# One pool of seven PSUM banks, handed out by the plan, in place of a ring of four and a ring of three

## The reference

```
h = layernorm(x) * (1 + ca) + sa
x = x + ga * attention(h)       # 16 heads of 16, causal, softmax
h = layernorm(x) * (1 + cb) + sb
x = x + gb * ffn(h)
```

## Time and profile before

| what | value |
|---|---|
| runs | 2794.85, 2794.88, 2792.37 us; median 2794.85 |
| the profiled execution: its own time | 2790.14 us |
| its span, first to last instruction | 2788.4 us |
| mean granted TensorE clock | 0.961 |
| instructions | 55137 |
| PE / DVE / ACT / POOL busy | 2464.7 / 2156.4 / 1711.5 / 1025.8 us |

### The profile page before, as it was taken

One profiled execution on the slowest core, in us unless ns is written; L12 is line 12 of the kernel. 1 busy time (PEld: TensorE's weight loads), 2 busy tenths in 40 slices (PEclk: granted clock), 3 DMA queues, 4 the chain that ended last, 5 costly groups with the idle time before them and its releaser, 6 DMA issues.

```text
span 2788.4 us, 55137 instructions
## 1 busy us (share of the span) xinstructions
PE 2464.7 (88%) x18968; PEld 1027.6 (37%) x18968; DVE 2156.4 (77%) x6588; ACT 1711.5 (61%) x3458; POOL 1025.8 (37%) x1558
## 2 busy tenths in 40 slices
PE   6898888988999999988999989999999989897686
PEld 4323333423334343343434333443433434333223
DVE  3897758788887988878887988878888788872961
ACT  3475575555765667756675666656677566664264
POOL 4222542244242443335243442434433352335222
PEclk9999999999999999999999999999999999998788
DMA  6510143121413222311423214131223114004000
GB/s 213 171 58 20 37 130 99 34 80 48 139 48 101 62 89 83 111 49 50 122 67 93 77 53 139 54 104 51 88 83 111 49 50 136 21 29 136 30 2 16
DMA packets 142394, 218.29 MB, mean 78 GB/s; under 512 B 21190, under 2 KB 62556, under 8 KB 142052
## 3 DMA queue, kind: packets, MB, share of 16 engines
q1 hardware_dynamic: 142120, 214.77, 25.5%
HBM read 137.87 MB, written 77.89 MB: 77 GB/s over the span
## 4 chain that ended last, share of the span: by engine, by line
PE 54%; DVE 24%; ACT 10%; issue 5%; POOL 5%; DMA 1%; SPq 0%; DVEq 0%; POOLq 0%; ACTq 0%
PE ctx_ps L1649 11%; PE big L1630 11%; PE big L1567 10%; DVE small L1398 8%; PE big L1556 8%; PE small L1608 7%; ACT probs L1184 6%; DVE mx L1396 4%; PE big L1681 4%; ACT xn L1233 4%; DVE stats L1352 3%; PE big L1664 2%; DVE region L1461 2%; DVE mx L1398 1%; DVE region L1499 1%
## 5 line engine op out<-in xcount | busy, mean ns | idle before, releaser
L1184 ACT ACTIVATE probs<-big 128x512 f32<-128x512 f32 (+2 forms) x2560 | 1221.4, 563 | 429.9 <-PE big L1630 421.4
L1398 DVE CUSTOM_DVE_ANT_0 small<-small,mask 128x128 f32<-128x128 f32 (+3 forms) x2048 | 942.9, 520 | 141.6 <-PE small L1608 130.7
L1630 PE MATMUL big<-stack_q,stack_k 64*128 64x512 f16 (+3 forms) x6144 | 711.8, 330 | 81.1 <-ACT probs L1184 52.8
L1396 DVE TENSOR_REDUCE mx<-small 128x1 f32<-128x512 f32 x1024 | 652.1, 682 | 102.8 <-PE small L1608 96.5
L1649 PE MATMUL ctx_ps<-probs,v_ones 128*17 128x512 f32 (+3 forms) x6144 | 646.6, 498 | 28.8 <-POOL probs L1063 19.3
L1063 POOL TENSOR_SCALAR_AFFINE_SELECT probs<-probs 128x512 f32<-128x512 f32 x512 | 329.0, 653 | 674.4 <-ACT probs L1184 674.1
L1608 PE MATMUL small<-stack_k,stack_q 64*128 64x512 f16 (+3 forms) x3072 | 458.0, 335 | 130.9 <-DVE mx L1398 76.0
L1630 PEld LDWEIGHTS big<-stack_q,stack_k 64*128 64x128 f16 x6144 | 232.0, 95 | 610.5 <-issue 356.5
L1608 PEld LDWEIGHTS small<-stack_k,stack_q 64*128 64x128 f16 x3072 | 128.9, 94 | 549.6 <-DVE mx L1398 248.7
L1398 DVE DVE_READ_ACCUMULATOR2_ANT mx<- 128x1 f32 x2048 | 286.2, 140 | 0.0
L1556 PE MATMUL big<-hT,w_qkv 128*128 128x512 f32 x512 | 274.3, 640 | 1.5 <-ACT probs L1184 1.4
(11 more groups left out here) (94 smaller groups left out, 1938.6 us busy)
## 6 DMA issues: line engine op xcount, KB each, us to landing
image<-region SPq DMA_DIRECT2D x192, 256.0 KB
stack_q<-image SPq DMA_DIRECT2D x64, 512.0 KB, 3.8
stack_k<-image SPq DMA_DIRECT2D x64, 512.0 KB, 4.7
lo_dram<-region SPq DMA_DIRECT2D x64, 256.0 KB
w_qkv<-wqkv SPq DMA_DIRECT2D x16, 768.0 KB, 6.4
x_res<-x SPq DMA_DIRECT2D x32, 256.0 KB, 3.5
stack_q<-lo_dram SPq DMA_DIRECT2D x128, 64.0 KB, 4.2
stack_k<-lo_dram SPq DMA_DIRECT2D x128, 64.0 KB, 5.2
```

Source lines behind the costliest of these rows:

```text
L1184: s.activation(probs[:, n % HELD, heads, q0:], big[:, at.slot(turn), 0:len(pairs) * width] .rearrange("p (h q) -> p h q", h=len(pairs)), A ...
L1396: last = v.reduce_max(to, held, AX)
L1398: last = v.tensor_tensor_reduce(out=held, in0=held, in1=mask[:, BANK - width:], scale=1.0, scalar=3.0 * NEG, op0=ALU.add, op1=ALU.max, acc ...
L1630: last = te.matmul(big[:, at.slot(at.turn() + parity), j * width:(j + 1) * width], stack_k[rows, c, g * PAIR_N + pair, kt * P:(kt + 1) * P ...
```

## The change

`big` becomes one PSUM tensor of seven banks, and `small` is a view of its last three, used by the start-up items alone. The plan chooses the bank of every turn and every `max` bank use: of those open, the one whose last reader ends first in the model. Turns may use all seven once the first `max` step has been placed. In the model a turn still waits until no more than three turns are unread before it, and a `max` use until no more than two (`MOST`); the kernel itself waits for the chosen bank alone. All banks have a `freed` semaphore, so a `max` step on PE waits for two semaphores where it waited for one, and the `join` on DVE waits for each bank that the group's last uses had. The constant `DMA_NS` is changed, and the pulls of `max`, `pre` and `post` get an addend by phase (`PHASES`: four groups in each of two layers; five values are not zero), so the order of the items changes as well.

```diff
-RING = 4
-SMALL = 3
+BANKS = 7
+ONCE_BANKS = 3
+MOST = {"turn": 4, "max": 3}
...
-SEEN, DMA_NS = 232.7037, 466.9094
+SEEN, DMA_NS = 232.7037, 407.8548
...
+PHASES = {"max": (0.0000, 0.0000, 0.0000, 0.0000, 0.0000, 0.0000, 0.0000, 0.0000), "pre": (-0.0748, 0.0000, 0.1675, 0.0000, 0.0000, 0.0000, 0.0000, 0.0000), "post": (0.0397, 0.0000, 0.0000, -0.2876, 0.0000, 0.0000, 0.0000, -0.0889)}
...
+    def open_to(self, use):
+        return range(BANKS if self.taken["max"] else BANKS - ONCE_BANKS) if use == "turn" else range(BANKS)
+
+    def bank_free(self, use, n=1):
+        own, first = self.ends[use], MOST[use] - n + 1
+        return max(sorted(self.banks[b] for b in self.open_to(use))[n - 1], own[-first] if len(own) >= first else 0.0)
+
+    def take_bank(self, use):
+        b = min(self.open_to(use), key=lambda b: self.banks[b])
+        self.taken[use].append((b, self.used[b]))
+        self.used[b] += 1
+        self.banks[b] = 1e18
+        return b
...
-            return max(own, self.ring[self.turn % RING], self.ring[(self.turn + 1) % RING])
+            return max(own, self.bank_free("turn", 2))
...
-            return max(self.at(("stack", unit, item[2])), self.small[self.step % SMALL], self.small[(self.step + 1) % SMALL])
+            return max(self.at(("stack", unit, item[2])), self.bank_free("max", 2))
...
+        phase = 4 * UNITS[scores[0][1]][1] + scores[0][2] if scores else 7
...
-            return cost - PULL[name] * (done * all_[name] - taken[name] + AHEAD[name] * all_[name] / N_UNITS)
+            ahead = AHEAD[name] + (PHASES[name][phase] if name in PHASES else 0.0)
+            return cost - PULL[name] * (done * all_[name] - taken[name] + ahead * all_[name] / N_UNITS)
...
-        return (self.turn() if turn is None else turn) % RING
+        return MODEL.taken["turn"][self.turn() if turn is None else turn][0]
...
-        return turn // RING
+        return MODEL.taken["turn"][turn][1]
...
-        return (self.own("max") + parity) % SMALL
+        return MODEL.taken["max"][self.own("max") + parity]
...
-        big = ctx.enter_context(nc.psum_tensor("big", [P, RING, BANK], f32))
+        big = ctx.enter_context(nc.psum_tensor("big", [P, BANKS, BANK], f32))
+        small = big[:, BANKS - ONCE_BANKS:]
...
-                    dve.wait_ge(s_freed, at.now("max", SMALL))
+                    for bank, use in dict(MODEL.taken["max"][:at.own("max")][-GROUP_STEPS:]).items():
+                        dve.wait_ge(freed[bank], use + 2)
...
-                    pe.wait_ge(s_freed, at.now("max", 2))
+                    for parity in range(2):
+                        bank, use = at.max_bank(parity)
+                        pe.wait_ge(freed[bank], use + 1)
```

More of the change, by code:

```diff
@@ L84, in piece_width @@
     return BANK if qt // 4 > blk else (qt % 4 + 1) * P
+GROUP_STEPS = 2 * PAIR_N * len(MAX_BANKS)
 LN_CHAIN, LN_GUESS = 18, 4
@@ L228, in __init__ @@
         self.free = {"PE": 0.0, "ACT": 0.0, "DVE": 0.0, "POOL": 0.0, "SP": 0.0}
-        self.ring, self.small, self.shape = [0.0] * RING, [0.0] * SMALL, None
-        self.turn = self.step = 0
+        self.banks, self.used, self.shape = [0.0] * BANKS, [0] * BANKS, None
+        self.taken, self.ends, self.opened = {"turn": [], "max": []}, {"turn": [], "max": []}, None
         self.ready, self.pipe = {}, 0.0
@@ L252, in needs @@
         if kind == "half":
-            return max(self.needs(item[2]), self.ring[self.turn % RING])
+            return max(self.needs(item[2]), self.bank_free("turn"))
         if kind == "score":
@@ L260, in needs @@
         if kind == "max":
-            return max(self.at(("stack", unit, item[2])), self.small[self.step % SMALL], self.small[(self.step + 1) % SMALL])
+            return max(self.at(("stack", unit, item[2])), self.bank_free("max", 2))
         if kind == "rows":
-            return max(self.at(("join", unit, item[2])), self.ring[self.turn % RING])
+            return max(self.at(("join", unit, item[2])), self.bank_free("turn"))
         own = {"proj": [("ctx", unit), ("scale", unit)], "turned": [("xn", unit)], "qk": [("h", unit), ("pre_loads", unit)], "value": [("h", unit)],
                "gate": [("mix", unit)], "key": [("mix", unit)], "y": [("h", unit), ("square", unit), ("scale", unit), ("bias", unit, 3)]}[kind]
-        bank = 0.0 if item in self.ready else self.ring[self.turn % RING]
+        bank = 0.0 if item in self.ready else self.bank_free("turn")
         return max(self.at(*own), bank)
@@ L334, in bank @@
     def bank(self, end):
-        self.ring[self.turn % RING] = end
-        self.turn += 1
+        b = self.take_bank("turn") if self.opened is None else self.opened
+        self.opened, self.banks[b] = None, end
+        self.ends["turn"].append(end)
     def play(self, item):
@@ L346, in play @@
             self.ready[item[2]] = 0.0
+            self.opened = self.take_bank("turn")
             self.free["PE"] = begin + pe_cost(item[2]) / 2
@@ L364, in play @@
                 cost = sum(piece_width(qt, blk) * 1.04 + 75 for qt, blk, _ in item[4])
-                self.small[self.step % SMALL] = self.run("DVE", end + SEEN, cost)
-                self.step += 1
+                b = self.take_bank("max")
+                self.banks[b] = self.run("DVE", end + SEEN, cost)
+                self.ends["max"].append(self.banks[b])
         elif kind == "rows":
@@ L685, in slot, with max_bank @@
     def slot(self, turn=None):
-        return (self.turn() if turn is None else turn) % RING
+        return MODEL.taken["turn"][self.turn() if turn is None else turn][0]
     def uses(self, turn):
-        return turn // RING
-    def small(self, parity):
-        return (self.own("max") + parity) % SMALL
+        return MODEL.taken["turn"][turn][1]
+    def max_bank(self, parity):
+        return MODEL.taken["max"][self.own("max") + parity]
     def done(self, item):
@@ L800, in adaln_program @@
         w_lin = w_ffn[:, 2]
-        big = ctx.enter_context(nc.psum_tensor("big", [P, RING, BANK], f32))
+        big = ctx.enter_context(nc.psum_tensor("big", [P, BANKS, BANK], f32))
+        small = big[:, BANKS - ONCE_BANKS:]
         ctx_ps = ctx.enter_context(nc.psum_tensor("ctx_ps", [P, BANK], f32))
-        small = ctx.enter_context(nc.psum_tensor("small", [P, SMALL, BANK], f32))
         c_in = sem("c_in")
@@ L824, in adaln_program @@
         filled = sem("filled")
-        freed = [sem(f"freed_{i}") for i in range(RING)]
+        freed = [sem(f"freed_{i}") for i in range(BANKS)]
         s_filled = sem("s_filled")
-        s_freed = sem("s_freed")
         xn_ready = sem("xn_ready")
@@ L1263, in _ @@
                 dve.sem_inc(bank, 1)
-            dve.sem_inc(s_freed, SMALL)
             dve.sem_inc(pv_done, HELD)
@@ L1392, in step @@
                             width = piece_width(qt, blk)
-                            held = small[:, at.small(parity), col:col + width]
+                            held = big[:, at.max_bank(parity)[0], col:col + width]
                             to = mx[:, g % 2, (parity * PAIR_N + pair) * NT + qt, blk:blk + 1]
@@ L1400, in step @@
                                     scale=1.0, scalar=3.0 * NEG, op0=ALU.add, op1=ALU.max, accum_out=to)
-                        last.then_inc(s_freed, 1)
+                        last.then_inc(freed[at.max_bank(parity)[0]], 1)
                 elif kind == "join":
                     g = item[2]
-                    dve.wait_ge(s_freed, at.now("max", SMALL))
+                    for bank, use in dict(MODEL.taken["max"][:at.own("max")][-GROUP_STEPS:]).items():
+                        dve.wait_ge(freed[bank], use + 2)
                     v.tensor_tensor(mxc[:, g % 2, :], mx[:, g % 2, :, 0], mx[:, g % 2, :, 1], ALU.max)\
@@ L1607, in step @@
                             rows = rows_of(parity)
-                            last = te.matmul(small[:, at.small(parity), col:col + width],
+                            last = te.matmul(big[:, at.max_bank(parity)[0], col:col + width],
                                              stack_q[rows, 0, g * PAIR_N + pair, qt * P:(qt + 1) * P],
```

## The result

| kernel | median us | runs | ratio to before, 95% interval |
|---|---|---|---|
| before | 2793.61 | 4 | |
| changed | 2745.93 (2741.7 to 2751.26) | 4 | 0.9833, 0.9812 to 0.9853 |

The forecast of 2755 us was 9 us too high; the change saves 48 us where 40 were forecast. The profiled execution took 2751.26 us, with a span of 2749.5; it is the slowest of the four. A ratio is worked out from all executions of the two kernels, the one before measured again beside each experiment, so it need not be the quotient of two medians.

A forecast was written before the change was run, and what follows sets the result against it. PE, near full, was taken to idle mostly for PSUM banks. The terms -38 - 3 + 2 = -39 us took 2790.1 us to 2751, or 2755 for the median; range 2705 to 2806, the forecast's own 2735 to 2785.

The forecast's parts named there:

- What bounds it: PE, busy 88%, idles 324 us, mostly waiting for banks: 126.5 us on DVE's reductions, 52.8 and 12.3 on ACT.
- Four fifths go on the spot, a third comes through: Steady part: of 144.1 us of PE's bank waits the pool ends 115 us; a third, 38 us, reaches the end.
- 38 + 3: Forecast pool gain in us: 38 from steady bank waits, 3 from scores' waits for ACT outside 100 to 2500 us.
- signs: DVE waits before max steps under 50 us, ACT waits before scores under 25, DVE idle before maxima down 20 or more.
- The edges: Outside 100 to 2500 us: max steps' 39.1 us of waits give 0 (far end 31), scores' 12.1 us give 3.
- Waits added: Second semaphore wait per max step on PE, 51 ns each, taken as 0; with the join's extra waits, 2 us lost.
- The join's term: Up to six more waits at 21 ns on DVE, 64 times: 8 us at most, taken as 2 us.
- A new order: Changed DMA_NS and PHASES reorder the items: taken as 0, with 22 us to either side.
- Rival 1: Nearly all ended bank waiting reaches the end: 100 us, 2695 us for the median; chance 0.15.
- rival 2: The waits move: PE, early, waits as long for data; 2795 us, within 0.2%; chance 0.12.
- Rival 3: Slower: turns on PE stand behind late maxima on DVE; 2827 us if 12% of 1175 turns wait; chance 0.18.
- The clock: Closing PE's short gaps may raise the granted clock; at 0.99 in the steady part, nothing was added to the sum.

The follow-up runs named there:

- own_pools_old_order: Changed kernel on the old item order, longest free bank chosen, but turns among four banks and max uses among three, nothing shared: 2806.89 us, ratio 1.0052 to before.
- pool_old_order_late_first: Changed kernel's pool of seven on the old item order, the later-freed of two bank waits put first: 2745.51 us, ratio 0.9841 to before.
- before_score_waits_swapped: Kernel before with the two bank waits of each score swapped, none added or dropped: 2777.6 us, ratio 0.995.
- the pair with the idle wait: Kernel before with an already met wait added to each max step, ahead of the bank's wait (2804.85 us, 1.0042) or after it (2793.39 us, 1.0001).

## Why the prediction was right, and where it was not

*What bounds it.* Right: the waits were for banks, on both sides, and a common pool took a good part of them away. own_pools_old_order shows that sharing is what does it.

*Four fifths go on the spot, a third comes through.* Both terms were off, in opposite directions. The kernel before and pool_old_order_late_first have one order, but they differ in the pool and in the place of the scores' waits, which is worth 15 us by itself. The pair that differs in the pool with its waits well placed on both sides is before_score_waits_swapped and pool_old_order_late_first. PE in the latter, whole run:

```profile
PE big L1639 <- DVE mx L1423: 38.1, 64, 3.7
PE big L1694 <- ACT xn L1259: 36.0, 10, 9.4
PE ctx_ps L1679 <- POOL probs L1089: 33.0, 28, 3.5
PE big L1639 <- DVE mx L1421: 30.3, 44, 3.5
PE big L1660 <- ACT probs L1210: 18.6, 25, 1.7
...
PE big L1660 <- DVE mx L1423: 13.2, 23, 2.1
...
PE big L1639 <- ACT probs L1210: 7.7, 23, 0.4
...
PE big L1660 <- DVE mx L1421: 3.8, 8, 1.4
PE big L1694 <- ACT probs L1210: 3.8, 6, 1.7
```

The bank waits in these rows are 115.5 us, where before_score_waits_swapped had 79.5 + 51.6 + 46.9 + 12.3 = 190.3: 75 us gone, two fifths of them and not four fifths. I had counted free banks as they stood in the old run. In the new one PE has already used them: it is early, and stands still again when the pool is empty. The same count on the changed kernel's timeline says so: of 136 us of bank waits, 34 could be ended by another bank, where it was 173 of 216. Of the 75 us about half reach the end, not a third: the span falls by 36 us (2778.7 to 2742.4), the median by 32. So the pool with its waits well placed on PE (the join's waits are in it) gave 32 us where my sum had 38 + 3, and against the kernel before, with the waits as the changed kernel has them, 28.

Only 13 us of the 36 are idle time of PE (318.2 to 305.1). The waits for data took back most of the rest, as foreseen: POOL's mask from 19.1 to 33.0 us, the normalised tiles from 20.6 to 36.0, the maxima's rows from 5.7 to 17.1, the context's own bank, which is not in the pool, from 9.0 to 17.2. (The highest data wait of the steady part in the kernel before was not the mask's 16.2 us, as I had written, but the 16.7 us of a gate for the mix, just above it.) The other 23 us are PE's busy time (2460.5 us in before_score_waits_swapped, 2437.3 in pool_old_order_late_first), which no step of mine had. The traces offer a reason that no run tests. Idle time in front of a PE instruction occurs 608 times in the one trace and 502 times in the other. The last matmul before such a break counts with its whole time, 355 ns on average, while inside a busy stretch one matmul starts 122 ns after another. An estimate from these numbers is 0.23 us of busy time for each break, 25 us for 106 of them. Over all fourteen traces busy time goes with the number of breaks (correlation 0.93), but not by this figure alone: the changed kernel has 523 breaks to 660 in the kernel before and only 13 us less.

Of what I named as signs, in the changed kernel, waits for ACT before scores fell below 25 us as said, those for DVE before max steps only to 88.6 where I had under 50, and DVE's idle time before maxima fell by 16.4 us where I had 20.

*The edges.* I gave the tail of max steps 0. Start of the first and last max step in the changed kernel, against the earlier trace rows:

```profile
L1634 PE MATMUL big<-stack_k,stack_q x3072: 212/372/632, 79.5 to 2663.1; 64*128 64x512 f16 x128, 64*128 64x128 f16 x64
```

The last starts 32.8 us earlier, so 33 of the 39 us of the span were won up to there and 6 behind. Outside 100 to 2500 us max steps wait 88.6 - 37.3 - 29.5 = 21.8 us instead of 39.1 (the changed kernel's rows for that stretch follow), so something was won there too. The stretches have shifted against the work, so how much can't be said. The scores' 12.1 us there are gone: all 14.9 us that are left lie between 100 and 2500 us.

```profile
PE big L1634 <- DVE mx L1421: 37.3, 73, 1.4
PE big L1634 <- DVE mx L1419: 29.5, 47, 2.9
```

*Waits added.* This step failed. I wrote that "the wait hides below the matmuls queued before it" and "If that cover is gone, after a stall, the step is late by 51 ns", and then summed it as 0. The cover is gone at each stall, about 200 of them, and the price there is 89 ns and not 51: 11.5 us in the pair with the idle wait. All the added semaphores together measured 18.6 us on rings, where my sum had 2. My argument that scores carry such a wait already, so that it must be harmless, was the fault turned round: they had been paying for it, 15 us. The join's term was too small as well: its separate waits take 50 ns and not the 21 I had read from another line, and DVE's idle time before the joins grows from 2.1 to 10.4 us in the changed kernel. So I had "DVE is waiting for its own last reduction then anyway" wrong too.

```profile
L1430 DVE TENSOR_TENSOR mxc<-mx 128x32 f32<-128x32 f32 x64 | 16.0, 249 | 10.4 <-issue 4.1 <-ACT probs L1208 2.5 <-DVE mx L1421 1.3
```

*A new order.* I took 0 with 22 us to either side; it gives 15 on rings and 14 on the pool with well placed waits. By medians, step by step: -15 (scores' waits well placed), -32 (pool), -14 (order), +14 (the waits' place in the changed kernel) = -47, where 48 were measured and 39 forecast. That the forecast came so near is in part luck: the pool as it stands in the changed kernel gave 28 us, and an order that I had put at nothing gave most of the rest.

*The rivals.* Rival 1 (2695) and rival 2 (2795) are out. Rival 3's mechanism is there, with 14.7 us of scores behind DVE's banks, about a third of the 41 us from which it would have decided; higher caps make it large.

*The clock.* In the steady part of the profiled execution the clock did not rise with the shorter idle time. Changed kernel, 900 to 2500 us (against the earlier trace rows):

```profile
900.00:2500.00 1600.00, 1477.87 (x11664) 618.06 (x11663) 1321.28 (x4021) 1051.34 (x2137) 634.03 (x943) 0.97 0.26 77
```

PE idles for 122 us there instead of 128, and the granted clock is 0.97 instead of 0.99; from 2500 us to the end it is 0.88 instead of 0.83. One trace is not enough to judge by: over the run this execution has 0.959, and the three faster ones of the same kernel 0.962 to 0.965, where the kernel before has 0.957 to 0.961 in all executions with a clock on record. So the mean clock is higher by some 0.004. The Trainium skill's rule that I cited ("TensorE: Matmul & The Clock Gate", section on cycling through PSUM banks), that short idle times cost clock as well, agrees in direction by these means and not by the steady part; no run separates what the clock gave.

## What to carry to other kernels

When an engine stands still for a buffer and the owner of another, idle set of buffers shares the memory, put them in one pool, but let the plan keep a reserve; filling it to the last one in the plan couples the streams. Count a wait where the engine stands still, not on average: of several waits on one instruction, the one that comes last belongs where it has no instruction of its own. A count of free buffers in the old trace was too high for what they end, here by half, since the faster kernel uses them up. And when two parts of a change are compared through a third run, make sure that the run does not carry an improvement of its own, as the scores' waits did here.

## What the runs showed of the hardware

On PE's queue the first of two waits of the program rides on the weight load, and the other becomes an instruction of 51 ns. From the end of DVE's read to the matmul that waited for it, the median is 57 ns when its wait rides and 146 ns when it is the separate one; for ACT's reads of a score's bank, 145 ns before the swap and 56 ns after it. A separate wait that has long been met costs nothing that can be measured (1.0001, 0.9992 to 1.001, with 1152 of them). Before the join on DVE the separate waits of the changed kernel take 50 ns each (192 of them).
